# An LSTM with a three-layer network behind it: portions of 8, 8, 8, 8, 16, 16 steps, equal shares per step, and x's leading part in eight banks

## The chip, the cores and the metric

One core of one Trainium2 chip runs the whole kernel as one program. The metric is the device time in microseconds (us) of one execution. The kernel before was run three times: 295.53, 295.74 and 296.14 us, median 295.74.

## The reference

Inputs are x (32 sequences of 64 steps, 256 features), a first hidden state (32 x 256), the LSTM's weights Wx, Wh (256 x 1024) and bias, and three matrices of booleans that stand for weights of +1 and -1. Cut to what matters:

```python
xW = einsum('ntd,dg->ntg', x, Wx) + b
def step((h, c), xw_t):
    a = xw_t + h @ Wh
    i, f, o = sigmoid(a[:, :256]), sigmoid(a[:, 256:512]), sigmoid(a[:, 512:768])
    g = tanh(a[:, 768:])
    c = f * c + i * g
    h = o * tanh(c)
hs = scan(step, (h0, 0), xW)                  # 64 steps, one behind the other
h = concatenate([hs, -hs], -1)
h = relu(s0 * (h @ sign(k0))) * 2             # 512 -> 1024
h = relu(s1 * (h @ sign(k1))) * 2             # 1024 -> 1024
out = x + s2 * (h @ sign(k2))                 # 1024 -> 256
```

The 64 steps of the scan depend on each other; x @ Wx doesn't depend on them, and the three layers need only the steps that they read.

## The kernel before, in words

Everything is kept transposed: features on the 128 partitions, (step, sequence) along the columns, 32 columns for each step. There are three kinds of work on TensorE (PE).

**The step.** `step(t)` in the tensor program issues 16 matmuls of 32 columns (L338, the low part of Wh with the high part of h) as soon as h's high part is there, and 16 of 64 columns (L347, the high part of Wh with both parts of h) when the low part is there. They go to the two PSUM banks G0 and G1. VectorE (DVE) adds x @ Wx (L667, L670), ScalarE (ACT) takes the tanhs (L508), DVE forms the cell (L672 to L679), ACT takes its tanh (L511), DVE multiplies (L683, h's high part in 16 bits), and forms the low part (L684, L686). Then the next step can start.

**x @ Wx**, tiles ("x", i, j): i is a quarter of the steps (16 steps, 512 columns), j one of 8 groups of 128 outputs. x and Wx are each split into two parts in fp32r, which ACT makes (L433, L448, high) and DVE (L531, L540, low). Each tile is 6 matmuls of 512 columns (L363): `x_matmul` takes their order from a tuple of (half k of the contraction, part of Wx, part of x). The tile is then emptied into the buffer xw with scale and bias, by ACT (`x_empty`, L457) or, for the tiles of X_DVE in quarter 0, by DVE (L555). Quarter 0 has to be whole before step 0's sum. Its tiles 0 to 5 take the banks WK0 to WK3, ACC0, ACC1; tiles 6 and 7 take WK0 and WK1 again, after tiles 0 and 1 have been emptied.

**The layers**, tiles (0, c, m), (1, c, m) and ("o", c, k): c is a portion of the steps from CHUNKS, here 8, 8, 16, 16, 16 steps, that is 256 or 512 columns. A tile of layer 0 is 4 matmuls, of layer 1 it is 16, of the output 4 (L380 and L393); all of them load their own 128x128 weights. For every tile of layer 0 or 1, ACT writes the high part of its relu (`layer_hi`, L474) and DVE the low part (`layer_lo`, L545); both read the tile's PSUM bank, and DVE waits for ACT. `y_add` (L550) makes the output of a portion from ACC0 and ACC1, and SP sends it out. `h1s` names where layer 0's results of a portion lie; portion 2 and portion 4 lie in the part of xw whose steps are over.

**The order around the change.** Each engine runs its own list in program order. The lists come from `make_plan`: `tile_order` writes down the order of all the tiles; for each step, `fill(t)` gives a credit in us, and matmuls are taken off the order while the credit is above 0.1 (the cost of one is 0.229 for x, 0.0135 times the portion's steps for a layer: 0.108 or 0.216), and while their inputs are there by the plan. PE issues `step(t)`, then the matmuls of `pe_plan[t]`, which run while DVE and ACT do the rest of the step. ACT issues its tanhs of step t, then the tiles of `act_plan[t]`; DVE its part of step t, then the pieces of weight preparation that are due (steps 3 to 5, 8, 10, 12, 13, 14) and at most two tiles of `dve_plan[t]`. A tile that ends less than 0.75 us of credit before the end of a step's share goes to DVE in the next one. What is left after step 63 is `pe_plan[64]`, the tail.

Four banks (WK0 to WK3) serve the tiles of x and of layers 0 and 1 in turn; a tile takes the one that came free first, and the plan lets it start only when that bank has been emptied.

**The start.** SP's queue issues, in this order, Wx's first two quarters, Wh in four, h0, the bias, Wx's last two quarters, the scales, and then x's quarters 1 to 3 with k0, k1, k2 between; ACT's queue issues the two halves of x's quarter 0. The largest entry of Wh and h0 sets a scale (L612 to L633, with one reduction over partitions on GpSimd), which ACT's 16-bit copies of Wh (L438), DVE's low parts (L536) and every emptied x tile wait for.

Of the kernel before, what the change touches and what calls it, by code (L numbers as in the profile page):

```python
# [18 lines left out]
NJ = 8  # L19
NQ = 4  # L20
NWK = 4
# [12 lines left out]
GROUPS = ((0, 4), (4, 8))  # L34
FLAT = "p a b c -> p (a b c)"

CHUNKS = ((0, 8), (8, 8), (16, 16), (32, 16), (48, 16))
NC = len(CHUNKS)

X_DVE = (5, 6, 7)  # L40

X2_STEPS = (1, 2)
W0_STEPS = (3, 4, 5)
# [4 lines left out]

def fill(t):

    return 2.3 if t <= 0 else 2.12 if t < 32 else 2.25 if t < 48 else 2.55


class Seen:
# [20 lines left out]
def tile_order():  # L75

    def second(c, first, last):
        part = []
        for m in range(first, last):
            part.append(((1, c, m), 16))  # L80
            if m >= 2:
                part.append((("o", c, m - 2), 4))
        return part

    def both(c, beside, share):
        part = []
        for m in range(8):
            part.append(((0, c, m), 4))
            part += beside[share * m:share * m + share]
        return part + beside[8 * share:]  # L90

    def begin(c):
        return [((1, c, 0), 10), (("o", c - 1, 6), 4), ((1, c, 0), 6), ((1, c, 1), 8), (("o", c - 1, 7), 4), ((1, c, 1), 8)]

    order = [(("x", i, j), 6) for i in (1, 2) for j in range(NJ)]
    order += both(0, [(("x", 3, j), 6) for j in range(NJ)], 1)
    for m in range(8):
        order += second(0, m, m + 1) + [((0, 1, m), 4)]
    for c in range(1, NC):
        order += begin(c) + second(c, 2, 6)  # L100
        if c < NC - 1:
            rest = [("o", c, 4)] * 4 + [(1, c, 6)] * 16 + [(1, c, 7)] * 16 + [("o", c, 5)] * 4
            order += both(c + 1, [(tile, 1) for tile in rest], 5)
    order += second(c, 6, 8)
    return order + [(("o", c, k), 2) for k in (6, 7, 6, 7)]


def make_plan():
# [3 lines left out]
    pe, act, dve = ([[] for _ in range(T + 2)] for _ in range(3))  # L112
    bank, before = {}, {}
    free = [(n, None) for n in range(NWK)]
    for j, n in enumerate((0, 1, 2, 3, 4, 5, 0, 1)):
        bank["x", 0, j] = n
        before["x", 0, j] = ("x", 0, j - 6) if j >= 6 else None
    free = [(2, ("x", 0, 2)), (3, ("x", 0, 3)), (0, ("x", 0, 6)), (1, ("x", 0, 7))]
    emptied = {("x", 0, j) for j in range(NJ)}
    todo = []  # L120

# [12 lines left out]
    order, done, piece, credit = tile_order(), {}, 0, 0.0  # L134
    left = order[0][1]
    for t in range(-1, T + 1):
        credit = min(credit, 1.0) + fill(t)
        finished, spent = [], 0.0
        while piece < len(order) and (t == T or credit > 0.1):
            tile = order[piece][0]  # L140
            if tile[0] != "o" and tile not in bank:
                bank[tile], before[tile] = free.pop(0)
            a = done.get(tile, 0)
# [30 lines left out]
        n = len(todo) if t >= T - 1 else 1 + (len(todo) > 1)  # L174
# [9 lines left out]
def lstm_ffn(nc, x_d, h0_d, wx_d, wh_d, b_d, k0_d, k1_d, k2_d, s_d, out_d):  # L184
    ctx = ExitStack()
    with ctx:
# [6 lines left out]
        def sem(name):  # L193
# [41 lines left out]
        w2 = k2[:, :].bitcast(F8).rearrange("p (k c) -> p k c", k=8)  # L235
        zero16 = zero[:, :].bitcast(F16)

        h1b = xw[:, 0:4].rearrange("p u j c -> p (u j c)").bitcast(F16)
        h1s = [f.rearrange("p (m a c) -> p m a c", m=8, a=2) for f in (
            h1[:, 0:4096], h1[:, 4096:8192], h1b, h1[:, :], h1b)]  # L240

        G = [pb("G0"), pb("G1")]
        ACC = [pb("ACC0"), pb("ACC1")]
        WK = [pb(f"WK{i}") for i in range(NWK)]
        TILE = WK + ACC

# [40 lines left out]
        def wait_x_out(e, tile):  # L289
            _, i, j = tile  # L290
            if i == 0 and j in X_DVE:
                e.wait_ge(x_dve, X_DVE.index(j) + 1)
            else:
                e.wait_ge(x_act, NJ * i + j + 1 - (len(X_DVE) if i else 0))

        block = ctx.enter_context(nc.Block())

        @block.sync
        def _(eng):
            e = Seen(eng)  # L300
            eng.dma_start(wx[:, 0:2], wx_d[:, 0:2]).then_inc(dwx[0], 16)
            eng.dma_start(wx[:, 2:4], wx_d[:, 2:4]).then_inc(dwx[1], 16)
            for g in range(4):
                eng.dma_start(wh[:, 2 * g:2 * g + 2], wh_d[:, 2 * g:2 * g + 2]).then_inc(dwh[g], 16)
            eng.dma_start(h0[:, :, :], h0_d).then_inc(dh0, 16)
            eng.dma_start(bias[:, :], b_d[:, :]).then_inc(db, 16)
            for g in range(2, 4):
                eng.dma_start(wx[:, 2 * g:2 * g + 2], wx_d[:, 2 * g:2 * g + 2]).then_inc(dwx[g], 16)
            eng.dma_start(sv[:, :], s_d[:, :]).then_inc(ds, 16)
            eng.dma_start(x[:, 1], x_d[:, 1]).then_inc(dx[0], 16)  # L310
            eng.dma_start(k0[:, :, :], k0_d).then_inc(dk0, 16)
            eng.dma_start(x[:, 2], x_d[:, 2]).then_inc(dx[1], 16)
            eng.dma_start(k1[:, :], k1_d).then_inc(dk1, 16)
            eng.dma_start(x[:, 3], x_d[:, 3]).then_inc(dx[2], 16)
            eng.dma_start(k2[:, :], k2_d).then_inc(dk2, 16)
            for c, (s0, n) in enumerate(CHUNKS):
                for mo in range(2):
                    e.wait_ge(y_made[mo], c + 1)
                    eng.dma_start(out_d[:, s0 // 16, mo, B * (s0 % 16):B * (s0 % 16 + n)], y_tile(c, mo)).then_inc(dy[mo], 16)
            for mo in range(2):  # L320
                e.wait_ge(dy[mo], 16 * NC)

        @block.tensor
        def _(eng):
            e = Seen(eng)

            def step(t):
                if t > 0:
                    hi, pair = h16[:, t - 1, :, 0], h16[:, t - 1]
                    e.wait_ge(hh_made, t)  # L330
                else:
                    hi, pair = hz[:, :, 0], hz[:, :, :, :]
                    e.wait_ge(hz_hi, 1)
                for g, (j0, j1) in enumerate(GROUPS):
                    for j in range(j0, j1):
                        e.wait_ge(wlo, j // 2 + 1)
                        for k in range(2):
                            eng.matmul(G[g][:, 64 * (j - j0):64 * (j - j0) + B], w16[:, 1, j, k], hi[:, k],  # L338
                                       start=j == j0 and k == 0, stop=False, skip_group_check=True)
                if t > 0:  # L340
                    e.wait_ge(hl_made, t)
                else:
                    e.wait_ge(hz_lo, 1)
                for g, (j0, j1) in enumerate(GROUPS):
                    for j in range(j0, j1):
                        for k in range(2):
                            ins = eng.matmul(G[g][:, 64 * (j - j0):64 * (j - j0 + 1)], w16[:, 0, j, k],  # L347
                                             pair[:, k].rearrange("p a b -> p (a b)"),
                                             start=False, stop=j == j1 - 1 and k == 1, skip_group_check=True)
                    ins.then_inc(gates[g])  # L350

            def x_matmul(tile, a):
                _, i, j = tile
                k, wp, xp = ((0, 0, 0), (1, 0, 0), (0, 1, 0), (1, 1, 0), (0, 0, 1), (1, 0, 1))[a]
                if wp:
                    e.wait_ge(wxl, j // 2 + 1)
                else:
# [57 lines left out]
            e.wait_ge(zeroed, 1)  # L415
            for n in range(WARM):
                eng.matmul(G[n % 2][:, 0:256], zero16[:, 0:128], zero16[:, 0:256], start=True, stop=True)
            for j in range(NJ):
                for a in range(6):
                    matmul(("x", 0, j), a)  # L420
            for t in range(-1, T + 1):
# [6 lines left out]
        def _(eng):  # L428
# [31 lines left out]
            def layer_hi(tile):  # L460
                layer, c, m = tile
                e.wait_ge(l_mm[layer], 8 * c + m + 1)
                if layer == 0 and c == 2:
                    e.wait_ge(added[1], 16)
                if layer == 0 and c > 2:
                    e.wait_ge(l_mm[1], 8 * (c - 1))
                if layer == 1 and m >= NH2:
                    e.wait_ge(o_mm, 7 * c + m - NH2 + 1)
                if layer == 1 and m < NH2 and c > 0:
# [3 lines left out]
                        e.wait_ge(acc_mm[1], c)  # L473
                eng.activation(layer_dst(tile, 0), layer_src(tile), ACT.Relu).then_inc(hi_made[layer])  # L474

            for k in range(2):
                eng.dma_start(x[:, 0, k], x_d[:, 0, k]).then_inc(dx0[k], 16)
            e.wait_ge(zeroed, 1)
            eng.activation(warm[:, :], zero[:, 0:NJ], ACT.Tanh)
            wx_hi(0)  # L480
# [3 lines left out]
            wx_hi(2)  # L484
            wx_hi(3)
            w_hi(0)
            x_empty(("x", 0, 0))
            w_hi(1)
            x_empty(("x", 0, 1))
            x_hi(1, 0)  # L490
            x_hi(1, 1)
            w_hi(2)
            w_hi(3)
            e.wait_ge(scaled, 7)
            eng.activation(hz[:, :, 0], h0[:, :, :], ACT.Copy, scale=scale_h0).then_inc(hz_hi)
            x_empty(("x", 0, 2))
            half_gain = eng.alloc_register("half_gain")
            e.wait_ge(scaled, 8)
            eng.reg_load(half_gain, sci[0:1, 6:7])
            x_empty(("x", 0, 3))  # L500
            x_empty(("x", 0, 4))
            for tile in act_plan[-1]:
                x_empty(tile)

# [20 lines left out]
        def _(eng):  # L525
# [111 lines left out]
            x_lo(1, 0)  # L637
            x_lo(1, 1)
            w_lo(2)
            w_lo(3)  # L640
            e.wait_ge(hz_hi, 1)
            eng.scalar_tensor_tensor(hz[:, :, 1], h0[:, :, :], scale_h0, hz[:, :, 0], ALU.mult, ALU.subtract).then_inc(hz_lo)
            e.wait_ge(biased, 1)
            for j in X_DVE:
                x_empty(j)

            for t in range(T):
                xst = xw[:, t // 4].rearrange("p j (t b) -> p j t b", t=4)[:, :, t % 4]
                tg, ti, tf, to = (tT[:, 64 * i:64 * i + 64] for i in range(4))
                v = [G[g][:, 0:256].rearrange("p (j h b) -> p j h b", h=2, b=B) for g in range(2)]  # L650
                if t % 16 == 0:
                    wait_x_out(e, ("x", t // 16, 4))
                    wait_x_out(e, ("x", t // 16, 7))
                if t == 0:

# [94 lines left out]
```

## Time and profile before

| | us |
|---|---|
| runs, median of 3 (lowest, highest) | 295.74 (295.53, 296.14) |
| the profiled execution, its own time | 296.18 |
| its span, first to last instruction | 294.4 |
| start of step 0 on PE (first L338) | 21.8 |
| start of step 1 | 25.1 |
| start of step 63 | 235.2 |
| last matmul ends | 291.1 |

The granted TensorE clock is 0.999 of the full 2.4 GHz over the span. PE stands as busy for 281.0 us (95%), DVE for 208.4 (71%), ACT for 114.2 (39%). Matmuls are pipelined: the recorded duration of one (some 0.38 us at 512 columns) is longer than the distance from one to the next (some 0.22), so the distance is what counts for a sum. All times of the text are counted from the span's start.

### The profile page before, as it was taken

To read this page: it belongs to the slowest core of one execution; us is meant where nothing else is said; L and a number is where in the kernel's file an instruction comes from. 1 tells how busy PE (TensorE), PEld (TensorE's weight loads), DVE (VectorE), ACT (ScalarE), POOL (GpSimd) and SP (SyncE) were. 2 spreads that over 40 slices of the span, in tenths; PEclk is the share of its full clock that TensorE was granted. 3 is DMA by queue.
4 is the path that set the end of the run, shared out by engine and by line. 5 is a ranking of instruction groups with operands and counts; after the bars stand their busy time and mean duration, and the time that the engine had idled before them with its cause. 6 is when DMAs were issued, how large, how long until landed. Compare 5 with 4: busy or idle time off the path is not lost.

```text
span 294.4 us, 7860 instructions
## 1 busy us (share of the span) xinstructions
PE 281.0 (95%) x3224; PEld 183.7 (62%) x3224; DVE 208.4 (71%) x843; ACT 114.2 (39%) x320; POOL 0.8 (0%) x7
## 2 busy tenths in 40 slices
PE   7989999999999999988999999999999999999995
PEld 5868777777788887866655555555555544444441
DVE  1887888888788888878888787788787764331012
ACT  4495657554543333234433323353323334211010
POOL 0000000000000000000000000000000000000000
PEclk9999999999999999999999999999999999999999
DMA  6950000000000001000001000000010000010001
GB/s 194 398 235 1 3 2 0 3 2 2 2 1 2 2 2 39 2 3 2 1 2 38 0 3 2 2 0 2 3 71 3 2 1 2 0 71 0 2 0 71
DMA packets 4212, 8.67 MB, mean 29 GB/s; under 512 B 848, under 2 KB 1360, under 8 KB 4048
## 3 DMA queue, kind: packets, MB, share of 16 engines
q1 hardware_dynamic: 3888, 7.64, 7.2%
q8 instruction: 25, 0.41, 0.6%
q10 hardware_dynamic: 288, 0.52, 0.5%
q14 instruction: 11, 0.09, 0.1%
HBM read 6.07 MB, written 2.10 MB: 28 GB/s over the span
## 4 chain that ended last, share of the span: by engine, by line
PE 42%; DVE 35%; ACT 15%; issue 3%; DMA 2%; SPq 1%; DVEq 0%; ACTq 0%
PE WK L380 25%; ACT tT L508 8%; DVE sT L667 7%; PE ACC L393 6%; PE G L338 5%; DVE h L545 5%; ACT tC L511 4%; PE G L347 4%; DVE uT L675 4%; DVE cD L677 4%; DVE h L683 3%; DVE aT L670 3%; DVE h L686 2%; DMA xw<-in_wx 2%; PE WK L363 2%
## 5 line engine op out<-in xcount | busy, mean ns | idle before, releaser
L380 PE MATMUL WK<-h,k 128*128 128x256 f16 (+1 forms) x544 | 93.5, 317 | 0.0
L380 PEld LDWEIGHTS WK<-h,k 128*128 128x128 fp8e5 x544 | 50.6, 98 | 28.5 <-issue 1.6
L508 ACT ACTIVATE tT<-aT 128x128 f32<-128x128 f32 x128 | 32.6, 302 | 90.2 <-DVE aT L670 88.3
L380 PE MATMUL WK<-xw,k 128*128 128x512 f16 x256 | 61.0, 379 | 0.0
L545 DVE SCALAR_TENSOR_TENSOR h<-WK,h 128x256 f16<-128x256 f32 (+1 forms) x64 | 34.1, 550 | 27.4 <-ACT h L474 27.4
L363 PE MATMUL WK<-xs,wxs 128*128 128x512 f32 x180 | 47.8, 405 | 1.7 <-ACT xw L457 0.9
L338 PEld LDWEIGHTS G<-h,w 128*128 128x128 f16 x1008 | 30.4, 96 | 27.6 <-DVE h L683 25.4
L338 PE MATMUL G<-h,w 128*128 128x32 f16 x1008 | 35.4, 177 | 7.3 <-DVE h L683 6.1
L474 ACT ACTIVATE h<-WK 128x256 f16<-128x256 f32 (+1 forms) x64 | 29.9, 479 | 31.3 <-PE WK L380 31.2
L380 PEld LDWEIGHTS WK<-xw,k 128*128 128x128 fp8e5 x256 | 24.3, 98 | 26.5
L347 PE MATMUL G<-h,w 128*128 128x64 f16 x1008 | 39.5, 192 | 0.0
L363 PEld LDWEIGHTS WK<-xs,wxs 128*128 128x128 f32 x180 | 32.3, 189 | 8.5 <-ACT xw L457 1.3
L667 DVE TENSOR_TENSOR sT<-G,xw 128x128 f32<-128x128 f32 x126 | 31.6, 285 | 7.1 <-PE G L347 6.7
L393 PE MATMUL ACC<-h,k 128*128 128x512 f16 (+1 forms) x160 | 34.7, 337 | 0.1
L347 PEld LDWEIGHTS G<-h,w 128*128 128x128 f16 x1008 | 33.2, 97 | 0.1
L670 DVE TENSOR_TENSOR aT<-G,sT 128x128 f32<-128x128 f32 x126 | 30.0, 279 | 0.0
L511 ACT ACTIVATE tC<-cD 128x64 f32<-128x64 f32 x64 | 16.4, 256 | 34.8 <-DVE cD L677 34.8
L683 DVE TENSOR_TENSOR h<-oP,tC 128x64 f16<-128x64 f32 x64 | 14.4, 225 | 13.8 <-ACT tC L511 13.7
L393 PEld LDWEIGHTS ACC<-h,k 128*128 128x128 fp8e5 x160 | 15.2, 98 | 12.6 <-DVE h L545 0.6
L672 DVE SCALAR_TENSOR_TENSOR vT<-tT 128x64 f32<-128x64 f32 x63 | 14.2, 225 | 11.3 <-ACT tT L508 11.3
L457 ACT ACTIVATE xw<-WK,biasS,sci 128x512 f32<-128x512 f32 x28 | 20.9, 766 | 0.5 <-PE WK L363 0.4
L545 DVE SCALAR_TENSOR_TENSOR xw<-WK,xw 128x512 f16<-128x512 f32 x16 | 10.7, 686 | 8.8 <-ACT xw L474 8.8
(57 smaller groups left out, 139.3 us busy)
## 6 DMA issues: line engine op xcount, KB each, us to landing
x<-in_x SPq DMA_DIRECT2D x3, 512.0 KB, 8.1
out_y<-x SPq DMA_DIRECT2D x6, 256.0 KB, 2.0
xw<-in_wx SPq DMA_DIRECT2D x4, 256.0 KB, 6.0
xw<-in_wh SPq DMA_DIRECT2D x4, 256.0 KB, 7.3
k<-in_k SPq DMA_DIRECT2D x1, 1024.0 KB, 10.1
x<-in_x ACTq DMA_DIRECT2D x2, 256.0 KB, 4.8
k<-in_k SPq DMA_DIRECT2D x1, 512.0 KB, 7.5
out_y<-x SPq DMA_DIRECT2D x4, 128.0 KB, 1.9
```

Of the source, the lines that this page charges most:

```text
L338: eng.matmul(G[g][:, 64 * (j - j0):64 * (j - j0) + B], w16[:, 1, j, k], hi[:, k], start=j == j0 and k == 0, stop=False, skip_group_check=True)
L347: ins = eng.matmul(G[g][:, 64 * (j - j0):64 * (j - j0 + 1)], w16[:, 0, j, k], pair[:, k].rearrange("p a b -> p (a b)"), start=False, stop= ...
L363: ins = eng.matmul(TILE[bank[tile]][:, :], wxs[:, wp, j, k], xs[:, i % 2, xp, k], start=a == 0, stop=a == 5)
L380: ins = eng.matmul(layer_src(tile), w, rhs, start=a == 0, stop=last)
L393: ins = eng.matmul(ACC[mo][:, 0:width(tile)], w2[:, k, 128 * mo:128 * mo + 128], h2[:, k % NH2, part, 0:width(tile)], start=k == 0 and par ...
L474: eng.activation(layer_dst(tile, 0), layer_src(tile), ACT.Relu).then_inc(hi_made[layer])
L508: eng.activation(tT[:, B * j0:B * j1], aT[:, j0:j1].rearrange("p j b -> p (j b)"), ACT.Tanh, scale=half_gain).then_inc(tanhed[g])
L511: eng.activation(tC[:, :, :].rearrange("p j b -> p (j b)"), cD[:, :], ACT.Tanh, scale=0.5).then_inc(c_tanh)
L545: eng.scalar_tensor_tensor(layer_dst(tile, 1), layer_src(tile), 0.0, layer_dst(tile, 0), ALU.max, ALU.subtract).then_inc(lo_made[tile[0]])
L667: eng.tensor_tensor(sT[:, j0:j1], v[g][:, :, 1], xst[:, j0:j1], ALU.add).then_inc(summed[g])
L670: eng.tensor_tensor(aT[:, j0:j1], v[g][:, :, 0], sT[:, j0:j1], ALU.add).then_inc(added[g])
L683: eng.tensor_tensor(h16[:, t, :, 0], oP[:, :, :], tC[:, :, :], ALU.mult).then_inc(hh_made)
```

## The change

CHUNKS goes from five portions to six; the third and fourth have 8 steps in place of one of 16. `fill` is new, and `tile_order` is written for the new portions: where the next portion has 8 steps, its layer-0 tiles are put between the layer-1 tiles of this one. Layer 0's results of the portions lie in other buffers, with other waits in `layer_hi`. Quarter 0 of x takes all eight banks (TILE now has G0 and G1, which the steps use later), its emptying is shared out in another order, its first two tiles take the products of the first half of the contraction ahead of the others, and the six products of every x tile stand in another order. At the start, x's second half moves from ACT's queue to SP's, and h0, the bias and the scales from SP's to ACT's.

```diff
-CHUNKS = ((0, 8), (8, 8), (16, 16), (32, 16), (48, 16))
+CHUNKS = ((0, 8), (8, 8), (16, 8), (24, 8), (32, 16), (48, 16))
-X_DVE = (5, 6, 7)
+X_ACT = (0, 7, 1, 2, 3)
+X_DVE = (6, 4, 5)
+X_BANKS = (0, 1, 2, 3, 4, 5, 6, 7)
 def fill(t):
-    return 2.3 if t <= 0 else 2.12 if t < 32 else 2.25 if t < 48 else 2.55
+    return 1.8 if t < 0 else 3.0 if t == 0 else 2.24 if t < 48 else 2.45
 # tile_order
-    for m in range(8):
-        order += second(0, m, m + 1) + [((0, 1, m), 4)]
-    for c in range(1, NC):
-        order += begin(c) + second(c, 2, 6)
-        if c < NC - 1:
-            rest = [("o", c, 4)] * 4 + [(1, c, 6)] * 16 + [(1, c, 7)] * 16 + [("o", c, 5)] * 4
-            order += both(c + 1, [(tile, 1) for tile in rest], 5)
-    order += second(c, 6, 8)
+    order += second(0, 0, 2)
+    for c in range(NC):
+        if c:
+            order += begin(c)
+        if CHUNKS[c + 1:] and CHUNKS[c + 1][1] == 8:
+            for m in range(2, 8):
+                order += second(c, m, m + 1)
+                order += [((0, c + 1, n), 4) for n in {2: (0, 1), 3: (2,), 4: (3, 4), 5: (5,), 6: (6, 7)}.get(m, ())]
+            continue
+        if c == NC - 1:
+            order += second(c, 2, 8)
+            continue
+        last = 7 if c == NC - 2 else 6
+        order += second(c, 2, last)
+        rest = [(tile, 1) for m in range(last, 8) for tile in [("o", c, m - 2)] * 4 + [(1, c, m)] * 16]
+        order += both(c + 1, rest, len(rest) // 8)
 # make_plan
-    for j, n in enumerate((0, 1, 2, 3, 4, 5, 0, 1)):
-        bank["x", 0, j] = n
-        before["x", 0, j] = ("x", 0, j - 6) if j >= 6 else None
-    free = [(2, ("x", 0, 2)), (3, ("x", 0, 3)), (0, ("x", 0, 6)), (1, ("x", 0, 7))]
+    for j in range(NJ):
+        bank["x", 0, j], before["x", 0, j] = X_BANKS[j], None
+    free = [(j, ("x", 0, j)) for j in range(NWK)]
 # buffers of layer 0's results, banks
-            h1[:, 0:4096], h1[:, 4096:8192], h1b, h1[:, :], h1b)]
+            h1[:, 0:4096], h1[:, 4096:8192], h1[:, 0:4096], h1[:, 4096:8192], h1b, h1[:, :])]
-        TILE = WK + ACC
+        TILE = WK + ACC + G
 # SP's queue
             eng.dma_start(wx[:, 0:2], wx_d[:, 0:2]).then_inc(dwx[0], 16)
+            eng.dma_start(x[:, 0, 1], x_d[:, 0, 1]).then_inc(dx0[1], 16)
             eng.dma_start(wx[:, 2:4], wx_d[:, 2:4]).then_inc(dwx[1], 16)
...
-            eng.dma_start(h0[:, :, :], h0_d).then_inc(dh0, 16)
-            eng.dma_start(bias[:, :], b_d[:, :]).then_inc(db, 16)
-            eng.dma_start(sv[:, :], s_d[:, :]).then_inc(ds, 16)
 # ACT's queue, then ACT's program
-            for k in range(2):
-                eng.dma_start(x[:, 0, k], x_d[:, 0, k]).then_inc(dx0[k], 16)
+            eng.dma_start(x[:, 0, 0], x_d[:, 0, 0]).then_inc(dx0[0], 16)
+            eng.dma_start(h0[:, :, :], h0_d).then_inc(dh0, 16)
+            eng.dma_start(bias[:, :], b_d[:, :]).then_inc(db, 16)
+            eng.dma_start(sv[:, :], s_d[:, :]).then_inc(ds, 16)
...
             w_hi(0)
+            w_hi(1)
             x_empty(("x", 0, 0))
-            w_hi(1)
-            x_empty(("x", 0, 1))
             x_hi(1, 0)
             x_hi(1, 1)
             w_hi(2)
             w_hi(3)
...
-            x_empty(("x", 0, 2))
+            x_empty(("x", 0, 7))
+            x_empty(("x", 0, 1))
...
+            x_empty(("x", 0, 2))
             x_empty(("x", 0, 3))
-            x_empty(("x", 0, 4))
 # PE: step 0 waits for the banks G0, G1; products of x; start
+                    wait_x_out(e, ("x", 0, 6))
+                    wait_x_out(e, ("x", 0, 7))
-                k, wp, xp = ((0, 0, 0), (1, 0, 0), (0, 1, 0), (1, 1, 0), (0, 0, 1), (1, 0, 1))[a]
+                k, wp, xp = ((0, 0, 0), (0, 1, 0), (0, 0, 1), (1, 0, 0), (1, 1, 0), (1, 0, 1))[a]
-            for j in range(NJ):
+            for a in (0, 3):
+                for j in range(2):
+                    for b in range(a, a + 3):
+                        matmul(("x", 0, j), b)
+            for j in range(2, NJ):
                 for a in range(6):
                     matmul(("x", 0, j), a)
 # layer_hi
-                if layer == 0 and c == 2:
+                if layer == 0 and c in (2, 3):
+                    e.wait_ge(l_mm[1], 8 * (c - 1))
+                if layer == 0 and c == 4:
                     e.wait_ge(added[1], 16)
-                if layer == 0 and c > 2:
-                    e.wait_ge(l_mm[1], 8 * (c - 1))
+                if layer == 0 and c == 5:
+                    e.wait_ge(l_mm[1], 8 * 4)
 # DVE's program
             w_lo(2)
+            e.wait_ge(biased, 1)
+            x_empty(6)
             w_lo(3)
...
-            e.wait_ge(biased, 1)
-            for j in X_DVE:
-                x_empty(j)
+            x_empty(4)
+            x_empty(5)
```

`wait_x_out` counts the tiles that ACT has emptied by their place in X_ACT.

## Rows read from the trace of the kernel before

**Rows 1.** The page's head and the first line of its part 1.
```profile
span 294.4 us, 7860 instructions
PE 281.0 (95%) x3224; PEld 183.7 (62%) x3224; DVE 208.4 (71%) x843; ACT 114.2 (39%) x320; POOL 0.8 (0%) x7
```

**Rows 2.** Windows: steps 1-8, 9-15, 16-31, 32-47, 48-62, then the rest.
```profile
25.07:51.09 26.02, 25.64 (x332) 20.14 (x331) 22.02 (x101) 16.68 (x42) 0.00 (x0) 1.00 0.01 2
51.09:75.08 23.99, 22.59 (x307) 17.07 (x307) 20.23 (x90) 12.62 (x37) 0.00 (x0) 1.00 0.01 2
75.08:127.23 52.15, 49.84 (x817) 42.30 (x817) 43.02 (x201) 19.72 (x73) 0.00 (x0) 1.00 0.02 7
127.23:181.69 54.46, 51.99 (x704) 31.76 (x705) 44.63 (x195) 19.59 (x64) 0.00 (x0) 1.00 0.02 7
181.69:235.23 53.54, 52.80 (x661) 30.22 (x662) 43.41 (x183) 19.16 (x61) 0.00 (x0) 1.00 0.03 12
235.23:294.40 59.17, 55.75 (x285) 25.26 (x284) 18.92 (x37) 11.89 (x22) 0.00 (x0) 0.99 0.05 18
```

**Rows 3.** The chain that ended last, in the tail: start, us, what.
```profile
240.74 12.95 PE WK L380 x60
...
291.14 0.75 DVE x L550
```

**Rows 4.** Timeline, steps 16 to 19: start, us, engine, line, operation, [idle before].
```profile
75.95 2.24 PE L380 MATMUL WK<-h,k 128*128 128x256 f16 x19
...
78.42 0.57 PE L338 MATMUL G<-h,w 128*128 128x32 f16 x16 [0.22 <-DVE h L683]
...
79.30 2.35 PE L380 MATMUL WK<-h,k 128*128 128x256 f16 x20
...
81.65 0.56 PE L338 MATMUL G<-h,w 128*128 128x32 f16 x16
...
81.90 0.75 DVE L545 SCALAR_TENSOR_TENSOR h<-WK,h 128x256 f16<-128x256 f32 x2
...
84.91 0.56 PE L338 MATMUL G<-h,w 128*128 128x32 f16 x16
```

**Rows 5.** Timeline of PE, step 59.
```profile
221.61 0.56 PE L338 MATMUL G<-h,w 128*128 128x32 f16 x16
...
222.48 2.75 PE L380 MATMUL WK<-h,k 128*128 128x512 f16 x12
```

**Rows 6.** Timeline: a piece of weights in step 13; step 54, whose next starts at 207.42.
```profile
64.68 0.68 DVE L598 SCALAR_TENSOR_TENSOR k<-k,sign 128x512 uint32<-128x512 uint32 x1
...
203.62 0.56 PE L338 MATMUL G<-h,w 128*128 128x32 f16 x16 [0.16 <-DVE h L683]
...
203.88 1.28 DVE L545 SCALAR_TENSOR_TENSOR h<-WK,h 128x512 f16<-128x512 f32 x2
...
207.42 0.57 PE L338 MATMUL G<-h,w 128*128 128x32 f16 x16 [0.16 <-DVE h L683]
```

**Rows 7.** Timeline of PE: steps 32 and 48, the first of a portion.
```profile
127.23 0.57 PE L338 MATMUL G<-h,w 128*128 128x32 f16 x16 [1.09 <-DVE h L683]
...
181.69 0.56 PE L338 MATMUL G<-h,w 128*128 128x32 f16 x16 [0.68 <-DVE h L683]
```

**Rows 8.** The start: one piece of the chain, then the timeline.
```profile
4.95 6.68 DMA xw<-in_wx
...
12.89 2.88 PE L363 MATMUL ACC<-xs,wxs 128*128 128x512 f32 x12
...
19.41 2.56 PE L363 MATMUL WK<-xs,wxs 128*128 128x512 f32 x10 [0.92 <-ACT xw L457]
...
20.20 1.52 DVE L555 TENSOR_SCALAR xw<-WK,sci,biasS 128x512 f32<-128x512 f32 x2
...
21.10 0.78 ACT L457 ACTIVATE xw<-WK,biasS,sci 128x512 f32<-128x512 f32 x1 [0.41 <-PE WK L363]
...
22.75 0.61 DVE L658 SCALAR_TENSOR_TENSOR sT<-G,sci,xw 128x128 f32<-128x128 f32 x2 [1.04 <-PE G L347]
```

More of the change, by code:

```diff
@@ L292, in wait_x_out @@
                 e.wait_ge(x_dve, X_DVE.index(j) + 1)
+            elif i == 0:
+                e.wait_ge(x_act, X_ACT.index(j) + 1)
             else:
-                e.wait_ge(x_act, NJ * i + j + 1 - (len(X_DVE) if i else 0))
+                e.wait_ge(x_act, NJ * i + j + 1 - len(X_DVE))
         block = ctx.enter_context(nc.Block())
@@ L650, in _ @@
                 v = [G[g][:, 0:256].rearrange("p (j h b) -> p j h b", h=2, b=B) for g in range(2)]
-                if t % 16 == 0:
-                    wait_x_out(e, ("x", t // 16, 4))
+                if t == 0:
+                    wait_x_out(e, ("x", 0, X_ACT[-1]))
+                    wait_x_out(e, ("x", 0, X_DVE[-1]))
+                elif t % 16 == 0:
                     wait_x_out(e, ("x", t // 16, 7))
```

## The prediction

> **What bounds the kernel now.** I read the page's head first, then the windows by stage, then one step of each kind in the timeline, and the start last. PE stands at 95% of the span [rows 1]; as matmuls overlap, that alone doesn't say that PE is the bound, so I worked out for each stage what PE has to do.
>
> Two limits set the length of a step. The **chain** (h, PE, DVE, ACT, DVE, h) takes 3.23 us from one step's first matmul to the next one's: 78.42 to 81.65 [rows 4]. **PE** needs 0.87 us for the step's own matmuls (221.61 to 222.48 [rows 5]) and one slot for each matmul of the fill. A wide slot (512 columns) is 12.95 / 60 = 0.216 us [rows 3], a narrow one (256 columns) 0.11, the difference between 19 and 20 of them [rows 4]. A slot of x is 0.24: step 0 has 10 and no idle time, from 21.81 to 25.07, so (3.26 - 0.87) / 10. A chain step thus has room for 11 wide, 21 narrow or 10 x slots at no cost.
>
> A third limit is DVE. It empties tiles between h's low part and the next sum. Two narrow tiles there take 0.75 us and the step is 3.26 long (81.65 to 84.91 [rows 4]); two wide ones take 1.28 and it is 3.79 [rows 6]. So what DVE does there beyond some 0.73 us lengthens the step by as much, unless PE is late by more.
>
> By these rules the five step stages of before come to 25.8, 23.9, 51.9, 54.3 and 53.4 us, against 26.02, 23.99, 52.15, 54.46 and 53.54 [rows 2], 0.9 short in all; the rules carry the sum, and I add each stage's shortfall again below. They also show where room goes unused: in steps 32 to 47, 16 x 0.87 + 48 narrow + 144 wide slots are 50.3 us of work in 54.46, and 16 to 31 hold 304 narrow slots, 47.4 in 52.15. PE sat idle for 1.09 and 0.68 us before steps 32 and 48 [rows 7], as the next portion's inputs weren't there, and the step after was overfull. From 48 to 62 PE is the bound (180 wide slots, 51.9 of 53.54): what is moved out of there only moves. Behind step 63 come its 12 slots and 240 more, a pure PE stretch.
>
> **The start.** Step 0's sum starts at 22.75, behind PE's step, which PE began at 21.81, after 10 fill matmuls that waited 0.92 for an emptied bank; DVE's last x tile is done at 21.72, ACT's at 21.88 with 0.41 of waiting in it [rows 8]. After the change, ACT still empties five tiles and DVE three, in an order that no longer waits for PE: x's splitting comes one emptying earlier for DVE, too. That puts the end of both at some 21.3 to 21.4, and the sum at 21.4. PE has tiles 4 to 7 of quarter 0 to do from about 12.65, when the low part of Wx's third quarter is there: 24 x 0.23 (2.88 for 12 with the drain of the last [rows 8]), so to 18.0. Then 6 slots, a wait for tile 1's bank until some 19.9 (it is ACT's third now), 2 slots, and step 0 at about 20.4. Its new waits for tiles 6 and 7, whose banks it uses, end at about 19.2, ahead of that. With 13 x slots in step 0 step 1 starts at 20.4 + 0.87 + 13 x 0.24 = 24.4, where it was 25.07: **-0.7 us**, with 21 fill matmuls done in place of 20. Bounds: +0.3 (the wait for tile 1 longer by a whole emptying of 0.78 [rows 8], and 0.2 more) and -1.6 (the start bound by the sum at 21.4 alone: the 1.35 that it gains, and 0.2).
>
> The DMAs moved: the third quarter of Wx is issued at 4.95 and lands 6.68 later [rows 8]. h0, bias and scales leave SP's queue (some 1.2 us of issuing ahead of it), and x's second half (0.4) joins. Read as issue time, the chain would give 0.8 us earlier landing. I take none, up to 0.3: the queue moved the same bytes ahead of it. The Trainium skill (DMA: Bandwidth & Descriptors, "Issuing engines are not separate DMA queues") says that DMAs of every issuing engine run on the same 16 DMA engines and interleave. By it the landing stays at 11.6. Either way PE's end of quarter 0 moves by less than 0.8 and then waits for ACT, so the sum changes by 0.2 at most.
>
> The other order of the six products, and the halves of tiles 0 and 1, let PE begin before x's second half is there; they cost nothing, as the next gate (Wx's third quarter) lies behind them. If that gate were gone they would save up to 0.8.
>
> **The steps.** Followed through the planner's rules (cost, credit, inputs, banks), the new constants give these slots, x / narrow / wide, before and after: steps 1 to 8: 74/0/0, 75/4/0; 9 to 15: 50/32/0, 48/46/0; 16 to 31: 0/304/0, 0/332/0; 32 to 47: 0/48/144, 0/331/0; 48 to 62: 0/0/180, 0/55/143; step 63 and tail: 252 and 241 wide.
> - 1 to 8: five steps at 10 x slots (3.26), three at 3.23, 0.1 for a step in which ACT has three tiles: 26.1.
> - 9 to 15: DVE has a piece of weights (0.68 [rows 6]) and two narrow tiles after step 10, so step 11 is 0.7 over; 12 to 15 are 0.1, 0.3, 0.3, 0.4 over, and step 9 is 0.2 over by PE. With the shortfall of 0.1: 24.8, that is 0.8 more than before.
> - 16 to 31: mostly 20 or 21 narrow slots, 3.23 to 3.25; step 27 has 25 (3.62), 30 has 24 (3.51). 52.6 + 0.25 = 52.85, 0.7 more than before, for 28 slots (3.1 us) more.
> - 32 to 47: 20 or 21 mostly; inputs are missing in steps 36 and 41 (12 slots each), and 37, 38 (24), 39, 44 (23) and 42 (29: 4.06) make up for it. 53.75, 0.7 less.
> - 48 to 62: 51.4, 2.1 less; 11 or 12 slots a step where it was 12, and double wide evacuations in fewer steps.
>
> In all 208.9 against 210.16: **-1.3**. Bounds: -3 (the misfits of steps 36 to 42 smooth themselves, since PE only waits for what is really missing) and +2 (below).
>
> **The tail.** 11 wide slots fewer: **-2.4** us. The last matmuls and the output stay as they are.
>
> **Costed at nothing.** 192 more matmuls load 192 more weights, 0.1 us each, on the load path; a narrow slot of 0.11 covers one just, and without that cover they would be 19 us. 32 narrow evacuations for 16 wide ones are some 2.4 us more of ACT and of DVE, in idle time except as counted. Two more output DMAs lie on SP, which waits anyway. The new waits in `layer_hi` are for tiles done long before: portion 0's layer 1 ends in step 23 and its buffer is written in 27, portion 1's in 33 and 36. Were one late, ACT would stand still ahead of the next tanh, and the chain with it.
>
> **Sum.** -0.7 - 1.3 - 2.4 = -4.4. The profiled execution took 296.18 (span 294.4, 1.8 around it), so 291.8; it was 0.44 above the median. On the median that is 295.74 - 4.3 = 291.4.
>
> **The rivals.**
> - *Pairs on DVE cost more.* Some 24 of the steps 16 to 47 have two narrow tiles on DVE; the rows give 0.02 each, as ACT is done in time. With ACT late by 0.1, each costs 0.1: +2.4, so 293.8. For it: the spare time is nil at 0.75. Chance 0.12.
> - *Slower: ACT late in every narrow step.* In steps 16 to 47 a tile that PE ends in its last slots makes ACT, then DVE, wait inside the chain. At 0.3 us a step, 31 steps give +9.3, so 300.7; it decides from 4.3 / 31 = 0.14 a step on. Against it: the planner defers such tiles on DVE, and the steps before with the same narrow slots ran at 3.26. Chance 0.05.
> - *More than forecast.* The start gives 1.6 and the steps 2 to 3: 289.9. Chance 0.10.
> - *It does nothing.* If PE's queue were the bound in all steps, the fill would be moved and no idle time removed; only the start would count, less its own slots: 295.4. The idle rows speak against it. Chance 0.03.
> - The forecast: 0.70, own range 290.3 to 292.8.
>
> A measurement of this kernel tells 0.2% (0.6 us) from no change. Faster holds the forecast, the first and the third rival: 0.92; same 0.03; slower 0.05. The range, 289.8 to 293.8, takes in those three.
>
> **What would show it.** Step 0 on PE at some 20.4, step 1 at 24.4; no idle of 1 us before steps 32 and 48; stage lengths as above (step 11 near 3.9, step 42 near 4.1); step 63 starting near 233.2, and the last matmul ending near 286.7, where it was 291.1. I am wrong if narrow steps stand at 3.35 or more, if Wx's third quarter lands after 12.2, or if the tail isn't shorter by 2.4.

## The result, and the profile after

The changed kernel took 291.6 us (median of 4 runs, 291.28 to 291.75) against 295.94 for the kernel before on the same chip (median of 4, 295.53 to 296.14: the three runs that stand above and one more of 296.14): ratio 0.9854, 95% interval 0.9836 to 0.9871. That is 4.3 us faster; the forecast was 291.4, with a range of 289.8 to 293.8. The profiled execution took 291.71 us with a span of 289.9.

First the page of the changed kernel, its head and the first line of part 1.

```profile
span 289.9 us, 8289 instructions
PE 280.0 (97%) x3416; PEld 202.1 (70%) x3416; DVE 209.2 (72%) x861; ACT 115.7 (40%) x336; POOL 0.8 (0%) x7
```

Against [rows 1] there are 192 more matmuls and weight loads, as there should be with twice as many narrow portions where a wide one was. PE's busy time is 1.0 us less and the span 4.5 less, so 3.5 us of what went was idle time of PE; the other 1.0 is in recorded durations, which overlap and are no measure of work. The weight loads took 18 us more on their own path, and PE's sum doesn't show them.

The windows by stage, cut at the same steps as [rows 2]: steps 1 to 8, 9 to 15, 16 to 31, 32 to 47, 48 to 62, and the rest. The columns are those of rows 2: the stretch, its length, then busy time and instructions of PE, PEld, DVE, ACT and POOL, the granted clock, DMA share and GB/s.

```profile
24.74:50.84 26.10, 25.97 (x337) 20.66 (x336) 21.48 (x95) 16.19 (x41) 0.00 (x0) 1.00 0.01 2
50.84:75.45 24.61, 23.83 (x318) 18.04 (x319) 20.59 (x91) 13.55 (x39) 0.00 (x0) 1.00 0.01 2
75.45:128.18 52.73, 51.83 (x845) 45.25 (x845) 44.20 (x205) 20.95 (x78) 0.00 (x0) 1.00 0.03 8
128.18:181.81 53.63, 51.58 (x845) 45.26 (x844) 45.09 (x207) 19.34 (x72) 0.00 (x0) 1.00 0.04 12
181.81:233.28 51.47, 50.73 (x679) 31.65 (x679) 42.65 (x185) 19.19 (x62) 0.00 (x0) 1.00 0.02 7
233.28:289.90 56.62, 53.23 (x273) 24.30 (x273) 18.52 (x36) 11.51 (x21) 0.00 (x0) 1.00 0.05 19
```

Stage by stage, in us:

| | before | forecast | after |
|---|---|---|---|
| step 1 starts at | 25.07 | 24.4 | 24.74 |
| steps 1 to 8 | 26.02 | 26.1 | 26.10 |
| steps 9 to 15 | 23.99 | 24.8 | 24.61 |
| steps 16 to 31 | 52.15 | 52.85 | 52.73 |
| steps 32 to 47 | 54.46 | 53.75 | 53.63 |
| steps 48 to 62 | 53.54 | 51.4 | 51.47 |
| step 63 to the last matmul | 55.9 | 53.5 | 53.35 |

Steps 9 to 15 and 16 to 31 got 0.6 us longer each. By the plan they took in 14 and 28 more narrow slots (and two of x fewer in the first of them); the 28 are worth 3.1 us of PE's time and cost 0.6. From step 32 on PE has less to do: the equal of 5 narrow slots less in steps 32 to 47, some 2 us of slots less in 48 to 62, and 11 wide ones fewer behind. Two details of the plan show one to one. The starts of steps 37, 38, 42 and 43 in the timeline of PE:

```profile
144.57 0.57 PE L350 MATMUL G<-h,w 128*128 128x32 f16 x16 [0.94 <-DVE h L706]
...
148.06 0.56 PE L350 MATMUL G<-h,w 128*128 128x32 f16 x16
...
161.41 0.56 PE L350 MATMUL G<-h,w 128*128 128x32 f16 x16 [0.91 <-DVE h L706]
...
165.46 0.56 PE L350 MATMUL G<-h,w 128*128 128x32 f16 x16
```

The idle time of [rows 7] before steps 32 and 48 is gone, but steps 36 and 41, which the plan leaves with 12 slots as the next inputs aren't there, leave 0.94 and 0.91 us idle at their ends, and step 42, with 29 slots, is 4.05 long (161.41 to 165.46).

### The profile page after: what moved, and what is told of

The parts are those of the page before. It is cut to its first block, busy times and chain, and to the rows that moved or that the text cites. A ratio compares the mean times of both kernels' runs of the same rounds, so it can differ in the third digit from the quotient of the medians.

```text
span 289.9 us, 8289 instructions
## 1 busy us (share of the span) xinstructions
PE 280.0 (97%) x3416; PEld 202.1 (70%) x3416; DVE 209.2 (72%) x861; ACT 115.7 (40%) x336; POOL 0.8 (0%) x7
## 4 chain that ended last, share of the span: by engine, by line
PE 67%; DVE 19%; ACT 8%; DMA 2%; issue 2%; SPq 1%; DVEq 0%
PE WK L392 35%; PE WK L375 8%; PE G L350 8%; PE G L359 7%; PE ACC L405 7%; ACT tT L528 4%; DVE sT L690 4%; DMA xw<-in_wx 2%; DVE h L565 2%; ACT tC L531 2%; DVE cD L700 2%; DVE uT L698 2%; DVE h L706 2%; DVE aT L693 2%; DVE xw L565 2%
## 5 line engine op out<-in xcount | busy, mean ns | idle before, releaser
L392 PE MATMUL WK<-h,k 128*128 128x256 f16 (+1 forms) x832 | 125.3, 297 | 0.0
L392 PEld LDWEIGHTS WK<-h,k 128*128 128x128 fp8e5 x832 | 78.6, 98 | 30.9 <-issue 1.9
L565 DVE SCALAR_TENSOR_TENSOR h<-WK,h 128x256 f16<-128x256 f32 (+1 forms) x88 | 41.1, 491 | 33.3 <-ACT h L492 33.3
L492 ACT ACTIVATE h<-WK 128x256 f16<-128x256 f32 (+1 forms) x88 | 36.7, 432 | 40.5 <-PE WK L392 40.3
L375 PE MATMUL WK<-xs,wxs 128*128 128x512 f32 x168 | 44.9, 405 | 0.2 <-ACT xw L473 0.2
L405 PE MATMUL ACC<-h,k 128*128 128x256 f16 (+1 forms) x192 | 36.5, 308 | 0.1
L392 PE MATMUL WK<-xw,k 128*128 128x512 f16 x128 | 31.1, 379 | 0.0
L405 PEld LDWEIGHTS ACC<-h,k 128*128 128x128 fp8e5 x192 | 18.1, 98 | 9.8 <-DVE h L565 0.6
L392 PEld LDWEIGHTS WK<-xw,k 128*128 128x128 fp8e5 x128 | 11.9, 98 | 12.5
L709 DVE TENSOR_TENSOR h<-h 128x64 f16<-128x64 f32 x64 | 14.4, 225 | 2.2
```

The costliest lines, as they stand in the source:

```text
L375: ins = eng.matmul(TILE[bank[tile]][:, :], wxs[:, wp, j, k], xs[:, i % 2, xp, k], start=a == 0, stop=a == 5)
L392: ins = eng.matmul(layer_src(tile), w, rhs, start=a == 0, stop=last)
L405: ins = eng.matmul(ACC[mo][:, 0:width(tile)], w2[:, k, 128 * mo:128 * mo + 128], h2[:, k % NH2, part, 0:width(tile)], start=k == 0 and par ...
L565: eng.scalar_tensor_tensor(layer_dst(tile, 1), layer_src(tile), 0.0, layer_dst(tile, 0), ALU.max, ALU.subtract).then_inc(lo_made[tile[0]])
```

## The experiments

Each was run five times (e2 and e9 eleven times) beside the kernel before, whose median was 295.9 to 296.0 us in every series. Ratios are to the kernel before, with 95% intervals.

**e1, the portions without the start.** The kernel before with CHUNKS, `tile_order`, `h1s`, `layer_hi` and the shares of the change from step 1 on, and nothing else (only the line of the shares is printed here):

```diff
-    return 2.3 if t <= 0 else 2.12 if t < 32 else 2.25 if t < 48 else 2.55
+    return 2.3 if t <= 0 else 2.24 if t < 48 else 2.45
```

> The kernel before with the six portions, their order, buffers and shares from step 1 on (2.24 and 2.45), and the start untouched. My theory (a step is as long as the longest of chain, PE slots and DVE's spare room) gives 207.2 us for steps 1 to 62 where it gives 209.5 for the kernel before, and 242 wide slots behind them in place of 252: -2.3 - 2.2 = -4.5 us, so 291.4, all of the whole change's saving. Rival: the start carries its share (0.7 us or more of the saving, as I forecast), and this run stays at 292.3 or above.

Measured: 291.33 us, ratio 0.9846 (0.9832 to 0.9859), no slower than the whole change. The rival, 292.3 or above, is out.

**e2, the start without the portions.** The changed kernel with the old portions, with their order, buffers and waits, and the old shares from step 1 on (only the line of the shares is printed):

```diff
-    return 1.8 if t < 0 else 3.0 if t == 0 else 2.24 if t < 48 else 2.45
+    return 1.8 if t < 0 else 3.0 if t == 0 else 2.12 if t < 32 else 2.25 if t < 48 else 2.55
```

> The changed kernel with the old five portions, their order, buffers and old shares from step 1 on; only the start is new. My theory: the steps' plan behind it is the same as before, so it saves what step 1 starts earlier, 0.3 us: 295.6. Rival (the start carries its share): 0.7 to 1.6 us, 294.3 to 295.2.

Measured: 295.70 us, ratio 0.9993 (0.9984 to 1.0002). The start alone can't be told from nothing. Together e1 and e2 settle where the saving is: in the portions with their shares. The smaller portions came with their own tile order and buffers, and no run takes these apart. In e2's profile the five stages are those of before (26.03, 24.06, 52.16, 54.46, 53.54).

**e3, new portions with the old shares.** The changed kernel with the share function of e2.

> The changed kernel with the old shares from step 1 on (2.12, 2.25, 2.55). By the slots: steps 1 to 62 as long as with the new shares (207.9), but 250 wide slots behind them in place of 241, as 16 steps take fewer each: 1.9 us slower than the changed kernel, 293.6, so 2.3 faster than before. Rival: PE is busy all the time, so shares only move work, and this is within 0.3 us of the changed kernel.

Measured: 293.24 us, ratio 0.9913 (0.9900 to 0.9927). By the medians the whole change divides into 0.2 us for the start (295.89 to 295.70), 2.5 for the portions with the old shares (to 293.24) and 1.6 for the new shares on top of them (to 291.6).

**e4, old portions with the new shares.**

```diff
-    return 2.3 if t <= 0 else 2.12 if t < 32 else 2.25 if t < 48 else 2.55
+    return 2.3 if t <= 0 else 2.24 if t < 48 else 2.45
```

> The kernel before with the new shares alone, portions as before. By the slots: steps 1 to 62 0.8 us shorter, but 259 wide slots behind them in place of 252 (1.5 us): 0.7 to 0.8 slower than before, 296.7, since the next portion isn't ready and credit is lost. Rival: equal shares save on their own, 1 us or more faster than before.

Measured: 298.62 us, ratio 1.0098 (1.0084 to 1.0112). The sign was right, the size was missed by 1.9. The same shares that save 1.6 us with the new portions cost 2.7 with the old ones. What I hadn't counted shows in windows of e4 around step 32 (columns as above; the clock is the third number from the end):

```profile
119.00:121.00 2.00, 1.78 (x17) 1.35 (x15) 1.57 (x9) 1.04 (x4) 0.00 (x0) 1.00 0.04 8
121.00:124.20 3.20, 1.04 (x32) 0.92 (x32) 2.56 (x13) 0.76 (x3) 0.00 (x0) 1.00 0.01 3
124.20:127.40 3.20, 1.04 (x32) 0.92 (x32) 2.56 (x13) 0.76 (x3) 0.00 (x0) 0.78 0.00 0
127.40:130.00 2.60, 2.53 (x35) 1.71 (x36) 1.51 (x8) 0.51 (x2) 0.00 (x0) 0.50 0.03 6
130.00:133.90 3.90, 3.90 (x18) 2.17 (x17) 1.83 (x9) 1.34 (x3) 0.00 (x0) 0.64 0.00 0
133.90:138.00 4.10, 4.08 (x77) 2.93 (x75) 3.35 (x13) 1.74 (x5) 0.00 (x0) 1.00 0.00 0
```

With 2.24 us a step the first two portions are used up after step 29, and the next one's inputs come with step 32. In steps 30 and 31 PE did its 32 step matmuls and nothing else (1.04 of 3.20 us busy in each of the two stretches); in the second of them the granted clock fell (its mean there is 0.78), it stood at 0.50, the lower of its two levels (1.2 GHz), in the stretch behind 127.40, and it came back to 1.00 in the one behind 130. The overfull step 32 ran through it and took 6.52 us (127.47 to 133.99).

**e9, the same with PE kept busy.** e4, with 20 matmuls of zeros into a free bank in each of the two empty steps; their results are overwritten by the next tile.

```diff
+                if 0 < t < T and not pe_plan[t]:
+                    first = (0, 2, 0)
+                    old = before[first]
+                    e.wait_ge(lo_made[old[0]], 8 * old[1] + old[2] + 1)
+                    for n in range(20):
+                        eng.matmul(WK[bank[first]][:, 0:256], zero16[:, 0:128], zero16[:, 0:256], start=True, stop=True)
```

> The kernel of e4 (old portions, new shares) with 20 matmuls of zeros in each of steps 30 and 31, whose plan is empty there; they go to a free bank and change nothing else. Theory: e4's extra 1.9 us over my slots came from TensorE's clock, which stood at half for 6.8 us behind two steps with 2.19 us of idle time each; with PE busy there the clock stays at 1.0 and the kernel takes 296.5 (e4 less 2.3 by its stage 32 to 47, 56.7 against 54.3 before). Rival: the clock had another cause and the time stays at 298.6.

Measured: 296.16 us, ratio 1.0015 (1.0006 to 1.0024). The timeline of PE in those steps, and the window of steps 32 to 47, of e9:

```profile
121.67 2.35 PE L429 MATMUL WK<-zero 128*128 128x256 f16 x20
...
124.91 2.35 PE L429 MATMUL WK<-zero 128*128 128x256 f16 x20
```

```profile
127.27:181.58 54.31, 52.34 (x705) 31.67 (x706) 44.39 (x194) 19.54 (x64) 0.00 (x0) 1.00 0.02 7
```

and the same stage of e4:

```profile
127.47:184.16 56.69, 54.73 (x705) 32.71 (x705) 44.53 (x194) 19.64 (x64) 0.00 (x0) 0.95 0.02 7
```

The same work with 40 useless matmuls ahead of it is 2.4 us shorter, and the clock stands at 1.00; step 32 takes 4.13 us in place of 6.52. The mean granted clock of the single runs agrees: 0.983 to 0.988 in all five of e4, 0.993 to 1.000 in the eleven of e9. So of e4's loss 2.5 us (298.62 to 296.16) are the clock. What is left over the kernel before is 0.3. In the profiles that is steps 1 to 62 shorter by 0.95 (209.21 for 210.16) and the rest, with 7 more wide slots, longer by 1.35 (57.23 for 55.88): without the clock the new shares still save nothing with the old portions.

**e5, other shares.** The changed kernel with shares that my rules for the length of a step put first:

```diff
-    return 1.8 if t < 0 else 3.0 if t == 0 else 2.24 if t < 48 else 2.45
+    return 1.8 if t < 0 else 3.0 if t == 0 else 2.2 if t < 16 else 2.3 if t < 32 else 2.24 if t < 48 else 2.55
```

> The changed kernel with shares of 2.2 us up to step 15, 2.3 up to 31, 2.24 up to 47, 2.55 behind. By my rules steps 1 to 62 take 207.6 us in place of 208.0 (9 to 15: 0.9 less, 16 to 31: 0.4 more, 32 to 47: 1.2 less, 48 to 62: 1.3 more), and 232 wide slots stand behind them in place of 241: 2.3 us faster than the changed kernel, 289.3. Rival: equal shares are what saves, and unequal ones are no better than the changed kernel, 291.6 or above.

Measured: 288.97 us, ratio 0.9767 (0.9754 to 0.9781): 2.6 us faster than the changed kernel where 2.3 was expected, and 7.0 faster than before. Equal shares aren't the best ones, and the rival is out. The windows of steps 9 to 15 and 32 to 47 of e5:

```profile
50.35:74.08 23.73, 23.12 (x314) 17.48 (x314) 20.23 (x90) 13.56 (x39) 0.00 (x0) 1.00 0.01 2
...
127.12:179.55 52.43, 51.86 (x847) 45.21 (x845) 44.53 (x206) 19.10 (x72) 0.00 (x0) 1.00 0.04 12
```

They are 0.88 and 1.20 shorter than the changed kernel's, as expected (0.9 and 1.2): step 10 no longer has two tiles and a piece of weights on DVE, and steps 36 and 41 aren't starved (23 and 20 slots for 12 and 12).

**e6, one piece of weights moved on DVE.**

```diff
-W1_STEPS = (8, 10, 12, 13)
+W1_STEPS = (8, 9, 12, 13)
```

> The changed kernel with DVE's second piece of k1's weights in step 9, where DVE empties one tile, in place of step 10, where it empties two. Theory (DVE beyond 0.73 us lengthens the step after it): step 11 falls from 3.83 to 3.3 and step 10 rises to 3.5, steps 9 to 15 0.6 us shorter, 291.0. Rival: step 11 is long for another reason (ACT's three tiles in it), and nothing changes.

Measured: 290.54 us, ratio 0.9811 (0.9798 to 0.9825). DVE and the step in the changed kernel, step 11:

```profile
57.83 0.68 DVE L618 SCALAR_TENSOR_TENSOR k<-k,sign 128x512 uint32<-128x512 uint32 x1
58.43 0.75 DVE L565 SCALAR_TENSOR_TENSOR h<-WK,h 128x256 f16<-128x256 f32 x2
59.10 0.48 DVE L690 TENSOR_TENSOR sT<-G,xw 128x128 f32<-128x128 f32 x2
```

and in e6:

```profile
57.27 0.83 DVE L565 SCALAR_TENSOR_TENSOR h<-WK,h 128x256 f16<-128x256 f32 x2
58.01 0.48 DVE L690 TENSOR_TENSOR sT<-G,xw 128x128 f32<-128x128 f32 x2
```

From the first DVE piece to the sum it is 1.27 us in the one and 0.74 in the other, and step 11 is 3.35 long in place of 3.83: the rival, by which nothing changes, is out. The expected cost in the new place (step 10 at 3.5) didn't come: step 10 is 3.27 in both. PE is late there by its own slots (step 9 is 3.49, and 3.50 in the changed kernel), and DVE's piece runs in that time. In e11 below, where step 9 is short (3.27), the same piece in the same place makes step 10 3.49 long, where it is 3.23 in e5. Steps 9 to 15 take 24.11 in place of 24.61. The medians differ by more than that (1.1 us); the rest is the start, of which more below: step 1 began at 24.19 in e6's profile and at 24.74 in the changed kernel's.

**e7, the DMAs as before.** The changed kernel with x's second half on ACT's queue and h0, bias and scales on SP's, in their old places.

```diff
-            eng.dma_start(x[:, 0, 1], x_d[:, 0, 1]).then_inc(dx0[1], 16)
+            eng.dma_start(h0[:, :, :], h0_d).then_inc(dh0, 16)
+            eng.dma_start(bias[:, :], b_d[:, :]).then_inc(db, 16)
```

(on SP; the reverse, with the scales, on ACT)

> The changed kernel with x's second half back on ACT's queue and h0, bias and scales on SP's. Theory: the landing of Wx's third quarter is set by the bytes ahead of it; it lands within 0.3 us of 11.2 to 11.8 and the time is within 0.3 us of the changed kernel's, 291.6. Rival: SP's issue time sets it, it lands 0.8 later, at 12.2 or so, and the kernel takes 292.3.

Measured: 291.21 us, ratio 0.9837 (0.9823 to 0.9850). The moved DMAs give nothing that can be seen. The Trainium skill (DMA: Bandwidth & Descriptors, "Issuing engines are not separate DMA queues") has the DMAs of all issuing engines interleave on the same 16 DMA engines; by that rule the landing stays, and the traces agree as far as their spread allows: ACT took up the third quarter of Wx at 11.33 in e7. In the four other profiles with the old DMA order (before, e1, e4, e9) it did so at 11.14 to 11.65, in the six with the new order (the changed kernel, e2, e3, e5, e6, e11) at 11.02 to 11.79. The rival's 12.2 stands in none.

**e8 and e10, Wx's third quarter earlier.** e8 issues it ahead of Wh's fourth; e10 also moves its low part on DVE ahead of the reduction of Wh's fourth. The part of e10's edit on DVE:

```diff
             for g in range(4):
+                if g == 3:
+                    wx_lo(2)
                 e.wait_ge(dwh[g], 16)
```

> The changed kernel with Wx's third quarter issued ahead of Wh's fourth. Theory A: PE's tile 4, which waits for the low part of that quarter, is the start's gate: it lands 0.65 us earlier, and step 1 starts up to 0.6 earlier, 291.0. Theory B: the scale, for which Wh has to be whole, is the gate as well (ACT and DVE empty the tiles 0.6 later): step 1 starts where it did or up to 0.6 later, 291.6 to 292.2. I lean to B, as ACT waited 0.76 us for PE in the changed kernel and has that to spare.

> The kernel of e8 with DVE's low part of Wx's third quarter ahead of its reduction of Wh's fourth, where in e8 it stood behind the reductions and began at 12.70 although the data was there at 10.24. Theory A: this low part is PE's gate; tile 4's eleven products begin at 11.7 in place of 13.43, and step 1 starts 0.6 us or more earlier than in e8 (25.04), 290.9. Theory B: what hangs on the scale (emptying by ACT and DVE) is the gate next, within 0.6: step 1 at 24.4 to 25.0, 291.2 to 291.6, no faster than the changed kernel.

Measured: e8 291.50 us, ratio 0.9846 (0.9833 to 0.9859); e10 291.28 us, ratio 0.9846 (0.9833 to 0.9860). In e8's profile ACT took the quarter up 1.5 us earlier than in the changed kernel's (11.79), and 0.8 earlier than in any profile with the changed kernel's DMA order, but DVE's low part of it stood behind the reductions in program order and PE's eleven matmuls waited for it:

```profile
10.26 0.63 ACT L450 ACTIVATE wxs<-xw 128x512 fp32r<-128x512 f32 x1 [3.06 <-DMA xw<-in_wx]
...
12.70 0.68 DVE L552 TENSOR_TENSOR wxs<-xw,wxs 128x512 fp32r<-128x512 f32 x1
...
13.43 2.81 PE L376 MATMUL ACC<-xs,wxs 128*128 128x512 f32 x11 [0.91 <-DVE wxs L552]
```

Step 1 began at 25.04 there; neither theory of e8 had that cause. With the low part moved too (e10) it began at 23.79, 1.25 earlier, yet the medians of the two kernels are 0.2 apart and both intervals hold the changed kernel's ratio. The profile of e10 speaks for theory A, its time (291.28) for theory B. The profiled execution of e10 is unlike the other four: it took 291.70 with a span of 288.8, so 2.9 us lay around the span, where it is 1.8 in the other four, whose spans are 289.1 to 290.1. As the changed kernel's are 289.5 to 289.9, those four show no earlier start beyond that spread. Why the profiled one has a short span and a long time stays open. A start that is earlier by the span's clock isn't by itself a shorter execution.

**e11, all of it.** Shares 2.2 / 2.3 / 2.24 / 2.6, k1's pieces as in e6, k2's in step 15.

> The changed kernel with shares 2.2 / 2.3 / 2.24 / 2.6, k1's pieces in steps 8, 9, 12, 13 and k2's in step 15, where no tile is emptied by DVE. My rules: 0.6 us less than e5, so 288.4, and 2.6 % faster than the kernel before. Rival: e5 has already taken what e6 gives, as its plan leaves step 10 with one tile: within 0.2 of e5, 289.0.

Measured: 289.08 us, ratio 0.9768 (0.9755 to 0.9781), the same as e5. My 288.4 was wrong and the rival's 289.0 right. Steps 1 to 62 took 207.99 together (e5: 207.87), and 3 wide slots fewer stood in step 63 and behind; but from step 63's start to the last matmul it took 51.57 us, as e5 did with 3 more. Two rows of e11's waits from 233 us on; in e5's the first stands at 0.5 us and the second doesn't stand:

```profile
PEld WK L392 <- DVE h L709: 1.1, 1, 1.1
PE WK L392 <- DVE h L709: 0.6, 1, 0.6
```

PE waited for the low part of the last h, without which layer 0 of the last portion can't start. Of the portion before, 9 slots are left for step 63 in e11 and 12 in e5, and neither covers the chain: from step 63's start to the first matmul of that layer 0 it is 3.62 us in e11 and 3.63 in e5. A slot taken out of step 63 then saves nothing. A share is worth spending only while something is left for the chain's last turn.

## Why the prediction was right, point by point

**The three limits of a step.** Chain, PE slots and DVE's spare room gave the five stages to within 0.2 us each (table above), 208.9 in all against 208.54 measured. The same rules had steps 1 to 62 at 207.2, 207.9 and 207.6 in e1, e3 and e5; the profiles show 207.71, 208.54 and 207.87, so they run 0.3 to 0.6 short, as they ran 0.9 short on the kernel before. They have no term for the granted clock, which cost e4 2.5 us, nor for the wait for the last h, and so missed e11 by 0.7. The surest one is DVE's: step 11 was put at 3.9, took 3.83, and e6 took it away by moving one piece.

**The tail.** 11 slots fewer were put at 2.4; from step 63's start to the last matmul it is 55.88 before and 53.35 after, 2.5 less. e1, with 242 slots behind step 62, has 53.56, and e5, with 232, has 51.57.

**How close, and by what luck.** The last matmul was put near 286.7 and ended at 286.64. That is closer than the terms: step 1 began 0.34 later than forecast, the steps took 0.36 less and the tail 0.15 less, and the three errors nearly cancel. Two of the prediction's sums are also loose, by less than 0.2 us: 24 products of 0.23 from 12.65 on end at 18.2 and not at 18.0, and the saving of 4.4 became 4.3 on the median.

**The start, the term that was off.** I put it at -0.7; step 1 began 0.33 earlier in the changed kernel's profile, and e2 as a whole saves 0.2, with an interval that holds none. The step that failed is "from about 12.65, when the low part of Wx's third quarter is there". The kernel before, then the timeline of the changed kernel:

```profile
12.31 0.69 DVE L531 TENSOR_TENSOR wxs<-xw,wxs 128x512 fp32r<-128x512 f32 x1 [0.48 <-ACT wxs L433]
```

```profile
11.79 1.27 ACT L449 ACTIVATE wxs<-xw 128x512 fp32r<-128x512 f32 x2 [4.75 <-DMA xw<-in_wx]
12.45 0.69 DVE L551 TENSOR_TENSOR wxs<-xw,wxs 128x512 fp32r<-128x512 f32 x1 [0.96 <-ACT wxs L449]
...
13.19 2.76 PE L375 MATMUL ACC<-xs,wxs 128*128 128x512 f32 x11 [0.23 <-DVE wxs L551]
...
18.71 0.78 ACT L473 ACTIVATE xw<-G,biasS,sci 128x512 f32<-128x512 f32 x1 [0.76 <-PE G L375]
...
20.21 0.73 PE L375 MATMUL WK<-xs,wxs 128*128 128x512 f32 x2 [0.18 <-ACT xw L473]
```

The low part was done at 13.14, as DVE takes 0.69 behind ACT's 0.63. In the kernel before it was done at 13.00, not 12.65, with ACT's take-up at 11.65: 0.35 of the error is in my reading of those rows, 0.14 is the later take-up. What hangs on it came 0.3 to 0.5 later than I had it: ACT waited 0.76 for tile 7, step 0 began at 20.79 (I had 20.4), step 1 at 24.74. The wait for tile 1's bank, which I had at half a microsecond, was 0.18 by the row above, and 0.3 if counted in slots, as I had. The mechanism was right (PE's quarter 0, then ACT's order), its first date wasn't. The new order of the products, which I costed at nothing, lets one product of tile 4 run ahead of that low part (at 12.47), where the old order has two that don't need it; no run tells what that slot is worth.

That date moves by itself. ACT took up the quarter at 11.79, 11.02 (e2) and 11.33 (e7), and step 1 began at 24.74, 24.02 and 24.33: 12.95, 13.00 and 13.00 later. The profiles of e3, e5, e6 and e11 give 12.99 to 13.03. In the kernel before it is 13.42 (11.65 to 25.07), and in e1, e4 and e9, which have the old start, 13.43 or 13.44. At an equal landing the new start is thus worth 0.4 us, and the landing moved by nearly twice that from one execution to the next; a single profile couldn't have told it. With a take-up at 11.3, as in most of these profiles, step 1 of the changed kernel would have begun at 24.3 by this distance (an estimate): that its profile shows 0.3 and not 0.7 is in part chance.

**The rivals.** Pairs of narrow tiles on DVE cost what the rows gave: steps 17 to 25, most of them behind a pair, take 3.22 to 3.27. No narrow step stood at 3.35 for ACT's sake, so the slower rival had no footing. Step 36 did stand at 3.39 with 12 slots; there DVE had the two pieces of an output (`y_add`, 0.87 us together) ahead of the sum, which is the DVE limit again. "It does nothing" is refuted by e1. "More than forecast" didn't come, since the start gave less, not more, and the gaps at steps 36 and 41 stayed; e5 shows that they were worth 1.2.

**What was costed at nothing** was hidden, as said: 192 weight loads, the longer use of ACT and DVE (1.5 and 0.8 us more in all), two more output DMAs. The new waits of `layer_hi` show in no step.

## What to carry to other kernels

Where a chain of steps leaves a fixed gap on the busiest engine, work out the gap from the trace in that engine's own slots, and fill each step at least to it: the planner's shares alone were worth 2.6 us between the changed kernel and e5, with as many instructions on each engine, in other steps. Filling beyond the gap lengthens the step, but only moves the work as long as the tail is pure PE work: e5's steps 48 to 62 are 1.1 us longer than the changed kernel's, and what is behind them 1.8 shorter. Smaller portions are worth their extra matmuls where a share would otherwise find no inputs; without them the same shares made this kernel slower, by 0.3 us at the full clock and by 2.7 with the fallen one. Put side work on the second engine where it has room, by step and not by total.

## What the runs showed that I hadn't expected

Two steps with PE busy for a third of the time (1.04 of 3.20 us each) brought TensorE's clock from 1.0 to 0.5 behind them, and that cost e4 2.5 us, where the same plan at the full clock (e9) is 0.3 slower than the kernel before. The kernel before had one step (31) with 10 narrow slots and 1.09 us idle [rows 7] and kept its clock. Matmuls of zeros in the gap bought it back. And one 256 KB DMA, which ACT took up at 11.0 to 11.8 us in profiles with the same DMA order, sets the start of the chain: with the new start step 1 began 12.95 to 13.03 us behind it in seven profiles, whatever its date.
